# Turns as transposes, biases merged, and the loop over the images written out

## The reference

```python
# layer 0, for each image (c = 192 channels; rows and cols of the image are sequences of 32 steps)
u = x @ Win.T + bin;  g = sigmoid(x @ Wg.T + bg)          # 16 states, for rows and for columns
h = h @ A + g*u                                            # scan over 32 steps, both directions
y = h @ Wout.T + bout + x @ Wskip.T + bskip                # rows and columns, both directions, summed, times 0.25
xn = channel layernorm(x);  h1 = gelu(xn @ g1_w.T + g1_b); g = sigmoid(h1 @ g2_w.T + g2_b)
x = g*y + (1-g)*x
# layer 1, tokens of an image (1024), 6 heads of 32
x = x + attention(layernorm(x))   # each token sees 33 neighbours and token 0; token 0 sees all; bias bo on the output
x = x + moe(layernorm(x))         # 4 experts of 192 -> 768 -> 192 with gelu, biases b1 and b2, the best 2 for each token
```

## Time and profile before

| | |
|---|---|
| median of three runs | 3681.26 us |
| the profiled execution | 3664.44 us, of which the span is 3662.6 us |
| granted TensorE clock, mean of the span | 0.901 |
| TensorE matmul busy | 3046.3 us, 83% |
| VectorE busy | 1904.2 us, 52% |
| ScalarE, GpSimd busy | 1062.0 us (29%), 825.1 us (23%) |
| the chain that ended last | TensorE 50%, issue 23%, VectorE 14%, GpSimd 6%, ScalarE 3% |

### The profile page before, as it was taken

One profiled execution on the slowest core, in us unless ns is written; L12 is line 12 of the kernel. 1 busy time (PEld: TensorE's weight loads), 2 busy tenths in 40 slices (PEclk: granted clock), 3 DMA queues, 4 the chain that ended last, 5 costly groups with the idle time before them and its releaser, 6 DMA issues.

```text
span 3662.6 us, 57020 instructions
## 1 busy us (share of the span) xinstructions
PE 3046.3 (83%) x19305; PEld 2180.7 (60%) x19305; DVE 1904.2 (52%) x5215; ACT 1062.0 (29%) x3287; POOL 825.1 (23%) x656
## 2 busy tenths in 40 slices
PE   0597878888889888888888888889888888988677
PEld 0465656666566666666566666656566665666444
DVE  4463636455554545555464555545555554545444
ACT  0131423232323323232332323233332323233222
POOL 0000111231212223131222213122222312222434
PEclk9697978989899899989989899998989899998889
DMA  3320103231222323123232312322232232323365
GB/s 48 93 68 13 54 13 86 53 78 47 46 79 58 82 52 90 39 50 84 48 80 55 87 54 39 90 41 78 56 86 58 46 80 41 84 51 81 91 159 112
DMA packets 272639, 242.38 MB, mean 66 GB/s; under 512 B 209020, under 2 KB 250462, under 8 KB 261728
## 3 DMA queue, kind: packets, MB, share of 16 engines
q1 hardware_dynamic: 211616, 147.12, 15.0%
q0 software_dynamic: 50880, 52.59, 8.9%
q10 hardware_dynamic: 9856, 38.80, 3.4%
HBM read 133.24 MB, written 73.59 MB: 56 GB/s over the span
## 4 chain that ended last, share of the span: by engine, by line
PE 50%; issue 23%; DVE 14%; POOL 6%; ACT 3%; DMA 1%; SPq 0%; POOLq 0%; DVEq 0%; ACTq 0%
PE PSUM L1444 9%; PE PSUM L1421 7%; POOL slots L663 4%; PE PSUM L1461 4%; PE PSUM L1384 3%; PE PSUM L1430 3%; PE PSUM L1463 3%; PE PSUM L1462 3%; PE PSUM L1507 2%; PE PSUM L1485 2%; ACT HF L772 2%; PE PSUM L1556 2%; PE PSUM L1573 2%; PE PSUM L1546 2%; PE PSUM L1381 2%
## 5 line engine op out<-in xcount | busy, mean ns | idle before, releaser
L1444 PE MATMUL PSUM<-XT,WB 128*128 128x512 f16 x2010 | 539.0, 402 | 43.0 <-DMA META<-slots 43.0
L801 ACT ACTIVATE PSPT<-PSUM,NMX 94x126 f32<-94x126 f32 x1056 | 366.3, 357 | 576.9 <-PE PSUM L1497 308.8
L678 POOL DMA_INDIRECT out_dram<-Y,META x228 | 367.8, 1613 | 726.5 <-DVE Y L1034 653.6
L1007 DVE TENSOR_SCALAR HHI<-HF 128x512 f16<-128x512 f32 x402 | 173.3, 431 | 660.8 <-ACT HF L772 659.6
L772 ACT ACTIVATE HF<-PSUM,WB 128x512 f32<-128x512 f32 x402 | 276.0, 687 | 760.8 <-PE PSUM L1444 756.1
L1461 PE MATMUL PSUM<-WB,HHI 128*128 128x192 f16 x1608 | 408.1, 254 | 18.9 <-DVE HLO L1010 17.6
L1485 PE MATMUL PSUM<-KBD,QT 128*94 128x378 f32 x704 | 352.6, 589 | 63.5 <-issue 53.6
L1463 PE MATMUL PSUM<-WB,HLO 128*128 128x192 f16 x1608 | 404.4, 251 | 0.0
L1462 PE MATMUL PSUM<-WB,HHI 128*128 128x192 f16 x1608 | 404.2, 251 | 0.0
L634 POOL TENSOR_TENSOR TR<-TV,MHALF 128x4 f32<-128x4 f32 (+1 forms) x48 | 59.4, 1238 | 1336.1 <-DVE TV L885 1336.1
L663 POOL DMA_INDIRECT slots<-XROW,IDX x256 | 250.5, 978 | 348.8 <-DVE IDX L1174 220.5
(11 more groups left out here) (268 smaller groups left out, 4743.7 us busy)
## 6 DMA issues: line engine op xcount, KB each, us to landing
WB<-weights SPq DMA_DIRECT2D x67, 1600.0 KB, 6.7
XR<-in_x ACTq DMA_DIRECT2D x16, 768.0 KB, 5.4
out_dram<-X ACTq DMA_DIRECT2D x32, 384.0 KB, 2.4
weights<-WB ACTq DMA_DIRECT2D x4, 1600.0 KB, 6.3
GUP<-TGU SPq DMA_DIRECT2D x256, 8.0 KB, 1.8
slots<-XROW,IDX POOLq DMA_INDIRECT x256, 2.4
out_dram<-Y,META POOLq DMA_INDIRECT x228, 3.6
HF<-in_w ACTq DMA_DIRECT2D x6, 384.0 KB, 4.7
```

Source lines behind the costliest of these rows:

```text
L678: pool.indirect_dma_start(out[:, :], bass.IndirectOffsetOnAxis(row, 0), Y[:, wslot(i, j), q, :], None, bounds_check=B * T + BS - 1, oob_is ...
L801: e = act.activation(PS[0:QS, n % 2, h, :], PSUM[0:QS, n % 2, h * KS:(h + 1) * KS], ACT.Exp, bias=NMX[:, b, n % 2, h:h + 1], accum_out=DEN ...
L1444: mm = pe.matmul(dst, WB[:, ws, w:w + 128], XT[:, xs, chunk, :], start=(n == 0), stop=(n == 4))
```

## The change

```diff
-                    for t in (WQ, WK, WV, WO, XS, QT):
+                    for t in (WQ, WK, WV, QT):
                         dve.memset(t[96:128], 0.0)
...
+                    link(dve.memset(QT[96:97], 1.0))
...
-            with sp.Fori(2, B - 1) as i:          # likewise on pool, act, dve and pe
+            for i in range(2, B - 1):
...
             for j in range(NSEL_END):
                 add(B, j, last_blocks=True)
+            pool.wait_ge(f["added"], upto("added", B, NSEL_END))
...
+                    pe.matmul(PSUM[:, 0, 0:2 * C], ONES3[:], ROWS3[:, 0:C].unsqueeze(1).broadcast_to((3, 2, C)),
+                              start=True, stop=False, skip_group_check=True)
                     for t in range(2):
...
-                        pe.matmul(PSUM[:, 0, col], H1T[:, tt // 4, :], WG2[:, tt % 4, :], start=True, stop=False)
-                        pe.matmul(PSUM[:, 0, col], ONES3[:], ROWS3[:, 0:C], start=False, stop=True)
+                        pe.matmul(PSUM[:, 0, col], H1T[:, tt // 4, :], WG2[:, tt % 4, :], start=False, stop=True,
+                                  skip_group_check=True)
...
-                    if k == 0:
-                        pe.matmul(dst, ONES3[:], WB[0:3, ws, W_B2:W_B2 + C].bitcast(BF16), start=(q % 2 == 0),
-                                  stop=False, skip_group_check=True)
+                    if k == 0 and q % 2 == 0:
+                        b2 = WB[0:3, ws, W_B2:W_B2 + C].bitcast(BF16)
+                        pe.matmul(PSUM[:, 6 + q // 2, 0:2 * C], ONES3[:], b2.unsqueeze(1).broadcast_to((3, 2, C)),
+                                  start=True, stop=False, skip_group_check=True)
...
-                        mm = pe.matmul(PSUM[0:KS, 2 + n % 2, h * QS:(h + 1) * QS], PS[:, n % 2, h, :],
-                                       EYE[:, 0:QS], start=True, stop=True)
+                        mm = pe.transpose(PSUM[0:KS, 2 + n % 2, h * QS:(h + 1) * QS], PS[0:QS, n % 2, h, :],
+                                          EYE[0:QS, 0:QS])
...
-                    mm = pe.matmul(PSUM[0:HC, at_bank, (b - b0) * QS:(b - b0 + 1) * QS],
-                                   OS[:, b, oh * HC:(oh + 1) * HC], EYE[:, 0:QS], start=True, stop=True)
+                    mm = pe.transpose(PSUM[0:HC, at_bank, (b - b0) * QS:(b - b0 + 1) * QS],
+                                      OS[0:QS, b, oh * HC:(oh + 1) * HC], EYE[0:QS, 0:QS])
...
-                        pe.matmul(dst, OT[:, j, c:c + 128], WO[:, j, :], start=(j == 0), stop=False)
-                    mm = pe.matmul(dst, ONES3[:], ROWS3[:, C:2 * C], start=False, stop=True)
+                        mm = pe.matmul(dst, OT[:, j, c:c + 128], WO[:, j, :], start=(j == 0), stop=(j == 1))
...
+    wo_rows = np.zeros((128 - HC, 2, C), f)
+    wo_rows[0, 0] = a["L1_attn_bo"]
```

More of the change, by code:

```diff
@@ L118, in hybrid_kernel @@
         XG = sb("XG", [128, 2, T])
-        XS = sb("XS", [128, 2, T])
+        XS = sb("XS", [HC, 2, T])
         GST = sb("GST", [HC, 2, 2, 6])
@@ L232, in hybrid_kernel @@
                     (EYE[:], eye), (GAVG[:], gavg), (PROJ[:], proj_w), (WG2[:], g2_wT),
-                    (WQ[0:HC], wq), (WK[0:HC], wk), (WV[0:HC], wv), (WO[0:HC], wo), (BQ[:], bq), (BK[:], bk), (BV[:], bv),
+                    (WQ[0:HC], wq), (WK[0:HC], wk), (WV[0:HC], wv), (WO[:], wo), (BQ[:], bq), (BK[:], bk), (BV[:], bv),
                     (B1[:], b1), (GB[:], gate_b), (GATEW[:], gate_w), (KON[:], consts),
@@ L703, in _ @@
             image(1)
-            with pool.Fori(2, B - 1) as i:
+            for i in range(2, B - 1):
                 image(i)
@@ L859, in _ @@
             experts(1, rest(1), conv(2))
-            with act.Fori(2, B - 1) as i:
+            for i in range(2, B - 1):
                 attention(i)
@@ L1296, in _ @@
             assert links[0] == LINKS_1, links[0]
-            with dve.Fori(2, B - 1) as i:
+            for i in range(2, B - 1):
                 links_from(LINKS_0 + LINKS_1 - 2 * LINKS + i * LINKS)
@@ L1628, in _ @@
             experts(1, rest(1), conv(2))
-            with pe.Fori(2, B - 1) as i:
+            for i in range(2, B - 1):
                 attention(i)
@@ L1704 @@
         scan_v=sv, scan_u=su, scan_a=sa,
-        wq=halves(a["L1_attn_Wq"]), wk=halves(a["L1_attn_Wk"]), wv=halves(a["L1_attn_Wv"]), wo=halves(a["L1_attn_Wo"]),
+        wq=halves(a["L1_attn_Wq"]), wk=halves(a["L1_attn_Wk"]), wv=halves(a["L1_attn_Wv"]), wo=np.concatenate([halves(a["L1_attn_Wo"]), wo_rows]),
         bq=vec(a["L1_attn_bq"]), bk=vec(a["L1_attn_bk"]), bv=vec(a["L1_attn_bv"]),
```

## The result

The changed kernel takes 3483.96 us (median of 4 runs, 3477.69 to 3509.16) against 3681.73 for the kernel before in the same session (4 runs, 3676.69 to 3685.27): ratio 0.9477, 95% interval 0.9428 to 0.9525. That is 198 us less where 222 were forecast, and 25 us above the forecast of 3459, inside its range. The profiled execution has a span of 3475.7 us against 3662.6, 186.9 less, at a mean granted clock of 0.884 against 0.901.

A forecast was written before the change was run, and what follows sets the result against it. Bound by TensorE (83% busy) alternating with short ScalarE and VectorE chains, plus stalls at loop jumps. 174 less 15% is 148; with 70 and 4, 222 off 3664.4 gives 3443, median 3459 us; range 3400 to 3550.

The forecast's parts named there:

- Jumps: Twelve jumps back of the image loop: written out, each saves 5.8 us of stall and low clock, 70 (60 to 76).
- Turns of the exponentials: In the attention, 66 turns an image as transposes: 0.17 us a full-clock block, 2.6 us an image (0 to 7.6).
- Turns of the result and output bias, behind the attention: Behind the attention: halved turns of the result save 0.9 us, dropped bias matmuls of four output tiles 1.6, per image.
- Rival 3: The attention falls to half clock as TensorE idles about 0.5 us a block: slower, 3729 us; chance 0.05.
- Rest: In `rest`, ahead of the scan: turns, output tiles and one expert bias save 3.3 us an image, capped by SyncE's moves.
- Gate bias and expert bias: Merged bias matmuls: gate 0.35 us a pair, 1.4 an image; expert 0.37 a block, 1.1 an image, 3.7 for last ten.
- The 15%: Taken off the 174 us of per-image gains, leaving 148, for gelus or hidden transfers that come late.
- Rival 2: Straight code must also be fetched and stalls in its midst: the 70 us of the jumps are lost, 3529; chance 0.05.
- Rival 1: VectorE and ScalarE take the gain: only jumps, last blocks and a third of the 174 gain, 3549 us; chance 0.14.
- rival 4: More gain than counted: low-clock stretches shorten too and turns gain near 0.4 us a block, 3395 us; chance 0.08.
- Rival 5: New transposes do not overlap, each costing 0.25 us instead of 0.109: 198 us, so 3657; chance 0.02.
- a mean clock well under 0.90 in the attention: Sign that would show the prediction wrong: TensorE's mean clock well under 0.90 in the attention.

The follow-up runs named there:

- undone last: The changed kernel with the loop over images 2 to 14 put back as a hardware loop, all other edits kept: 3618.45 us, ratio 0.9831.
- the loop alone: The kernel before with only the loop over images 2 to 14 written out on all five engines: 3663.18 us, ratio 0.9969.
- The filled kernel: The changed kernel with matmuls of constants in TensorE's waits from attention block 6 to the output's turns: 3431.01 us, ratio 0.9313; on the second chip 3629.3.
- the kernel with every wait filled: The changed kernel with turns between the groups of scores and constant matmuls in TensorE's waits, also at blocks 1 to 3: 3377.34 us, ratio 0.9173.

## Why the prediction came out as it did

The direction was right and the size nearly so. In profiled executions 186.9 us went where 222 had been summed, and 35 us are to be found. That the median is off by 25 only is luck: this time the runs lie 8 us above the profiled span and not 19.

- **Jumps.** 12 x (4.47 + 1.52) = 72 us by the table, 70 forecast. But this holds only beside the other edits, and both its numbers are read from the kernel before; alone the loop brings 14. The sum treated the terms as independent, and they are not: undone last, it is worth 134.
- **Turns of the exponentials.** 2.5 us an image in the attention, 2.6 forecast, but of two errors that cancel. A block at full clock gains 0.33, not 0.17. Up to the start of `values` it is 0.18, as forecast (2.80 from the block's start, 2.98 in the earlier trace rows). The other 0.15 comes inside `values` (1.03 to the next scores, not 1.18), whose second half, it seems, waited for the second copy; the two copies now follow each other at once (0.80 for both). The attention's last stretch runs at half clock and gives part of it back; filled, it gains 3.4. The 2.5 also holds the 1.5 that the attention loses when the stall goes: against the loop alone it is 4.0. Back as matmuls they cost 25 us in all.
- **Turns of the result and output bias, behind the attention.** *This is the step that failed.* 0.9 + 1.6 = 2.5 an image was worked out at the full clock of the earlier trace rows; measured is -0.3 in image 4, since the stage now runs mostly at half clock. Over images 0 to 14 the two stages together are 0.8 us longer, where after the 15% taken off everything 15 x 2.1 = 32 less had been forecast: 33 us, nearly the whole gap. The other terms miss by less and cancel: all else together brings 188 of 190. The filled kernel shows the same stage at full clock with 2.56 gained. Rival 3 had the mechanism, but put it in the attention's middle, where the full clock holds.
- **Rest.** 2.5 instead of 3.3. The turns went from 3.36 to 1.80 us, as forecast, and the four output tiles from 4.0 to 2.7 (start to start), a little less. But five matmuls of an expert, which lay under the copies before, are late next, at half clock. The chain after (start, us, what):

```profile
817.88 1.80 PE PSUM L1551 x10
819.69 0.33 PE PSUM L1592 x12
820.01 2.11 PE PSUM L1448 x5
822.12 2.60 PE PSUM L1561 x16
...
829.84 2.17 PE PSUM L1355 x19
```

  From the turns' end to the outputs it is 2.4 us, where the kernel before had 1.55 (853.29 to 854.84, behind the turns of the earlier trace rows). The moves of the states, forecast as the cap, are not what ends last: the chain runs through TensorE.
- **Gate bias and expert bias.** 3.1 an image between the scan and the next scores, the stall left out; 2.5 forecast. A pair's mix at full clock spans 2.85 us instead of 3.34, 0.49 less where 0.35 had been forecast. The last ten blocks are 0.42 shorter each (0.37 forecast). Four pairs and three blocks make 3.2. The chunk with biases takes 1.63 us (2.05 in the earlier trace rows, 1.7 forecast):

```profile
3345.32 0.33 PE L1464 MATMUL PSUM<-WB,ONES 3*128 3x384 bf16 x1 [0.77 <-DVE Y L1036]
...
3346.95 1.24 PE L1448 MATMUL PSUM<-XT,WB 128*128 128x512 f16 x5
```

- **The 15%** had been taken for gelus and transfers coming late; none was found of that size, and it paid for a part of the clock instead. Without it the forecast would have been 3433, 51 us off.

Rival 2 is refuted: no stall of microseconds stands in the straight code. Rival 1 (VectorE and ScalarE take the gain, 3549) is wrong as a bound: neither engine has less to do in the filled kernel, and yet 54 us more go. Its mechanism is real in the attention, where TensorE now waits 126.9 us for VectorE's copy instead of 52.8; the prediction had counted that. Of rival 4 the shorter turns came in part (0.33 a block), the shorter stretches of half clock did not. Rival 5 is refuted by the six records in 0.65.

One sign of being wrong was badly chosen: "a mean clock well under 0.90 in the attention". It was 0.85 there before the change and is 0.88 after (image 4). The clock fell behind the attention, from the turns of the result to the projection: 1.00 before, 0.55 after.

The Trainium skill ("TensorE: Matmul & The Clock Gate", Part 4: PE-mode transpose) says that transposes don't count for the clock as matmuls do. The run with the exponentials' turns as matmuls bears on it: with 66 transposes an image made matmuls again the outputs stay at half clock in twelve of 13 images (the turns just ahead of them, still transposes, in ten). The loop alone, in which all these turns are matmuls, falls to half clock there as well, and the filled kernel, in which all 88 are transposes, does not. So here it is at most a small part. That TensorE's idle time ahead matters is shown by the filled kernels; what exactly the clock follows, and why images 6 and 11 of the loop alone stay at full clock beside eleven like them, stays open.

## What to carry to other kernels

Where TensorE's clock falls to half in places, price an edit only together with the stretch behind it: an edit that leaves TensorE waiting more can be paid for at half clock a few microseconds later, and edits that look independent are not (the same loop is worth 14 us alone and 134 undone last). Before cutting more work, look at the granted clock just behind each wait; here 54.6 us came from running useless matmuls in waits, on an engine that is busy 80% of the span. And measure a part both ways, put alone into the old kernel and taken alone out of the new one; either alone would have misled.

## What the runs showed of the hardware

- The stall of TensorE at a loop's jump isn't fixed: 4.5 us in the kernel before, 7.7 in the changed kernel with the loop back, 5.8 in one run with a load of 768 KB started later. What sets it is open.
- Chips differ by some 5.4% on the same kernel (3881 us on the second chip, 3677 and 3682 on the other two). In the four kernels profiled on the second chip, VectorE stands idle for some 10 us in the attention while GpSimd issues its gathers (eight of them in the row below), and ScalarE and TensorE wait for it. The profile gives no instruction that ends this wait ("remote"). Image 8 of the filled kernel there, its timeline:

```profile
1844.66 0.98 POOL L664 DMA_INDIRECT slots<-XROW,IDX  x1 [0.30 <-issue]
...
1846.03 0.35 DVE L1053 TENSOR_TENSOR XW<-PSUM,RDEN 94x192 f32<-94x192 f32 x1 [9.81 <-remote]
```

  The attention takes 59 to 66 us there instead of 46 to 54. I had laid this to the clock in the expectation of the kernel with every wait filled; the clock does fall in that image, but as the hole begins, and stays low some 8 us behind it; most of the added length is the hole's. No run on the other two chips has such a row, and its cause stays open.
